# Bias rows and key mask of two attention layers: from one-row fp32 matmuls to one matmul of three or six bf16 rows per bank

## What is computed

```
# layer 0 (8 heads of 32)
xn = LN(x)
q = softmax(xn @ Wq + bq, within a head)
k = softmax(xn @ Wk + bk + (1 - mask) * -1e6, over the tokens)
v = (xn @ Wv + bv) * mask
y = q @ (k^T v per head)
hh = silu(LN(y) * (1 + scale) + shift) @ W_out + b_out
x = x + hh
# layer 2 (16 heads of 16)
q = xn @ q_w + q_b;  k = xn @ k_w + k_b
att = softmax(q k^T + (1 - mask) * -1e6, over the keys)
y = att @ ((xn @ v_w + v_b) * mask)
hh = silu(LN(y) * (1 + scale) + shift) @ out_w + out_b
x = x + hh
```

## Time and profile before

| | us |
|---|---|
| median of 3 runs | 3865.28 (3852.82 to 3866.88) |
| the profiled execution, its span | 3873.2 |
| TensorE busy | 2902.1 (75%) |
| VectorE busy | 2801.5 (72%) |
| ScalarE busy | 2089.7 (54%) |
| GpSimd busy | 1716.0 (44%) |

### The profile page before, as it was taken

How to read it: one execution, slowest core, us unless ns; L and a number is a source line. 1 busy time by engine, 2 the same in 40 slices (tenths; PEclk the granted TensorE clock), 3 DMA queues, 4 the chain that set the end, 5 groups by cost and what they waited for, 6 DMA issues and landing times. The chain is left out here.

```text
span 3873.2 us, 38272 instructions
## 1 busy us (share of the span) xinstructions
PE 2902.1 (75%) x11060; PEld 1488.6 (38%) x11060; DVE 2801.5 (72%) x3410; ACT 2089.7 (54%) x3166; POOL 1716.0 (44%) x1209
## 2 busy tenths in 40 slices
PE   6999667877777877468788878866776866867775
PEld 4555333444444444222333322223434434434443
DVE  1333279999999999755555555515999989999996
ACT  0223267777777777213444444426766756767663
POOL 0000047678677768800000000003767667677686
PEclk7899787988988988768888888768887978878888
DMA  2000111111011101043333333010101011111011
GB/s 78 11 33 22 47 39 44 39 44 50 28 44 50 50 23 55 33 82 63 60 39 66 66 61 61 12 58 33 43 24 60 30 53 50 39 45 61 23 55 49
DMA packets 101857, 176.64 MB, mean 46 GB/s; under 512 B 10219, under 2 KB 88827, under 8 KB 92563
## 3 DMA queue, kind: packets, MB, share of 16 engines
q1 hardware_dynamic: 97430, 161.65, 15.8%
q0 software_dynamic: 4224, 12.59, 1.0%
HBM read 139.69 MB, written 34.12 MB: 45 GB/s over the span
## 5 line engine op out<-in xcount | busy, mean ns | idle before, releaser
L965 POOL TENSOR_TENSOR l_h<-l_h,l_c_all 128x512 f32<-128x512 f32 x1024 | 1483.1, 1465 | 709.6 <-DVE l_h L896 688.5
L896 DVE TENSOR_TENSOR_SCAN l_h<-l_dA,l_ps_dbu 128x512 f32<-128x512 f32 x1024 | 1210.1, 1205 | 137.2 <-PE l_ps_dbu L1089 81.8
L1089 PE MATMUL l_ps_dbu<-ident,l_dub 128*128 128x128 f32 x4096 | 691.8, 303 | 282.8 <-DVE l_h L896 256.9
L767 ACT ACTIVATE l_dub<-l_duT,l_b_tok 128x512 f32<-128x512 f32 x1024 | 723.6, 711 | 281.5 <-PE l_ps_dbu L1089 281.5
L1089 PEld LDWEIGHTS l_ps_dbu<-ident,l_dub 128*128 128x128 f32 x4096 | 520.2, 154 | 783.0 <-DVE l_h L896 535.5
L781 ACT ACTIVATE l_dA<-l_dt,l_a_neg 128x512 f32<-128x512 f32 x1024 | 724.1, 711 | 0.2
L1076 PE MATMUL l_ps_y<-l_h,ident 128*128 128x512 f32 x1024 | 630.2, 702 | 104.5 <-DVE l_h L864 103.9
L1346 DVE TENSOR_REDUCE l_q_max<-l_ring 128x2 f32<-128x1024 f32 x256 | 312.7, 1224 | 335.7 <-PE l_ring L1614 332.9
L1499 ACT ACTIVATE l_probs<-l_ring 128x1024 f32<-128x1024 f32 x256 | 261.7, 1024 | 433.3 <-PE l_ring L1623 432.3
L864 DVE TENSOR_TENSOR l_h<-l_h 128x512 f32<-128x512 f32 x512 | 459.8, 901 | 26.1 <-POOL l_h L965 26.0
L925 POOL DMA_INDIRECT l_x_in<-x_dram,l_idx_x x32 | 33.2, 1038 | 951.8 <-DMA l_idx<-in_idx 938.7
(11 more groups left out here) (181 smaller groups left out, 3049.2 us busy)
## 6 DMA issues: line engine op xcount, KB each, us to landing
l_c_all<-c_rows_dram SPq DMA_DIRECT2D x64, 1024.0 KB, 4.8
l_res<-x_dram SPq DMA_DIRECT2D x24, 512.0 KB, 5.4
parts_dram<-l_parts SPq DMA_DIRECT2D x48, 256.0 KB, 2.8
l_qs<-parts_dram SPq DMA_DIRECT2D x48, 256.0 KB
l_ks<-parts_dram SPq DMA_DIRECT2D x48, 256.0 KB
l_x_in<-x_dram SPq DMA_DIRECT2D x16, 512.0 KB, 5.3
x_dram<-l_res SPq DMA_DIRECT2D x16, 512.0 KB, 3.0
su_cond_w<-in_cond_w SPq DMA_DIRECT2D x1, 5120.0 KB, 15.1
```

The lines of the kernel that those rows point to most:

```text
L767: return act.activation(dub[:, n % 2, t, :], duT[:, p, t, :], ACT.Copy, scale=b_tok[:, p, t, n:n + 1])
L896: dve.tensor_tensor_scan(h[:, h_slot(s), :], dA[:, s % DA_RING, :], ps_dbu[:, dbu_slot(s), :], 0.0, ALU.mult, ALU.add).then_inc(scan_ok, 1)
L965: pool.tensor_tensor(h[:, h_slot(s), :], h[:, h_slot(s), :], c_all[:, (n // C_GROUP) % 2, n % C_GROUP, :], ALU.mult).then_inc(hc_ok, 1)
L1089: last = pe.transpose(ps_dbu[:, dbu_slot(s), t * P:(t + 1) * P], dub[:, n % 2, t, j * P:(j + 1) * P], ident[:])
```

## The change

Before, each bias was added by fp32 matmuls with one row. Now each bias is split into three bf16 parts whose sum is the fp32 value (first part: the value rounded to bf16; second: the rest rounded; third: the rest of that), the parts lie on three partitions (`row_stack`), and one bf16 matmul with three rows of ones as weights adds them to a whole bank of two token tiles. It now stands first in the bank and starts it (start=True); the fp32 matmuls add to it. For k of layer 0, bias and mask go into one matmul of six rows: the left side holds three bias parts over three rows of ones, the right side three rows of ones over three mask parts.

The parts are made once. For layer 0 that happens in the setup: VectorE splits, SyncE moves the parts onto their partitions, the mask's by way of memory. For layer 2 it happens at the layer's start. The load of the rows and the per-batch mask load and mask operation of layer 0 are gone.

```diff
 # setup_block, SyncE
+                sp.dma_start(mask_rest[:], io["mask_k"]).then_inc(mask_in, 16)
                 sp.dma_start(cond_w[:], io["cond_w"]).then_inc(weights_in, 16)
+                sp.wait_ge(mask_split, 5)
+                sp.dma_start(io["mask_parts"], mask_parts[:]).then_inc(mask_st, 16)
+                sp.wait_ge(split, 4)
+                for a in range(3):
+                    sp.dma_start(row_stack[a:a + 1, :], row_parts[:, a, :]).then_inc(stack_in, 16)
+                sp.wait_ge(ones_in, 3)
+                for a in range(3):
+                    sp.dma_start(k_left[a:a + 1, :], row_parts[:, a, D:2 * D]).then_inc(stack_in, 16)
+                sp.wait_ge(mask_st, 16)
+                sp.dma_start(k_right[3:6, :, :], io["mask_parts"].rearrange("b a t -> a b t")).then_inc(stack_in, 16)
+                sp.wait_ge(stack_in, 16 * 7)
                 sp.wait_ge(gate_out, 1)
 # setup_block, GpSimd
+                pool.memset(early["ones_b"][:], 1.0).then_inc(ones_in, 1)
+                pool.memset(k_left[:], 1.0).then_inc(ones_in, 1)
+                pool.memset(k_right[:], 1.0).then_inc(ones_in, 1)
 # setup_block, VectorE, ahead of its wait for TensorE
                 dve.wait_ge(loaded, 48)
+                dve.wait_ge(mask_in, 16)
+                dve.tensor_copy(row_parts[:, 0, :], rows[:, 0:4 * D]).then_inc(split, 1)
+                dve.tensor_scalar(mask_rest[:], mask_rest[:], 1.0, MASKED, ALU.subtract, ALU.mult).then_inc(mask_split, 1)
...
+                dve.tensor_tensor(mask_parts[:, 2, :], mask_rest[:], mask_parts[:, 1, :], ALU.subtract).then_inc(mask_split, 1)
 # linear_attention
-                sp.dma_start(rows[:], io["rows"]).then_inc(w_in, 16)
-                        sp.dma_start(mask_row[:, p, :], io["mask_k"][bass.ds(b, 1), :]).then_inc(mask_ld[p], 16)
-                    dve.wait_ge(mask_ld[p], loads)
-                    dve.tensor_scalar(mask_add[:, p, :], mask_row[:, p, :], 1.0, MASKED, ALU.subtract, ALU.mult).then_inc(madd_ok, 1)
-                def project(dst, src, weight, bias):
-                    for t in range(TB):
-                        for k in range(DH):
-                            pe.matmul(dst[:, t, :], src[:, k, t * P:(t + 1) * P], weight[:, k, :], start=(k == 0), stop=False)
-                        last = pe.matmul(dst[:, t, :], ones[:], bias, start=False, stop=True)
+                def project(bank, src, weight, bias):
+                    for a in range(2):
+                        pe.matmul(bank[:, a, :].rearrange("p (i d) -> p i d", d=D), ones_b[0:3, :], bias, start=True, stop=False, skip_group_check=True)
+                        for i in range(2):
+                            t = 2 * a + i
+                            for k in range(DH):
+                                last = pe.matmul(bank[:, a, i * D:(i + 1) * D], src[:, k, t * P:(t + 1) * P], weight[:, k, :], start=False,
+                                                 stop=(k == DH - 1), skip_group_check=True)
                     return last
-                        pe.matmul(ps_k[:, h, :], row("L0_bk")[:, h * P:(h + 1) * P], ones[0:1, 0:1].to_broadcast([1, T]), start=False, stop=False)
-                        last = pe.matmul(ps_k[:, h, :], ones[:], mask_add[:, p, :], start=False, stop=True)
+                        last = pe.matmul(ps_k[:, h, :], k_left[:, h * P:(h + 1) * P], k_right[:, bass.ds(b, 1), :], start=False, stop=True)
 # softmax_attention, SyncE, ahead of its wait for the mask parts
-                sp.dma_start(rows[:], io["rows"]).then_inc(w_ld, 16)
+                sp.dma_start(rows[:], io["rows"][:, 4 * D:6 * D]).then_inc(rows_ld, 16)
+                sp.wait_ge(split_ok, 4)
+                for a in range(3):
+                    sp.dma_start(row_stack[a:a + 1, :], row_parts[:, a, :]).then_inc(row_stack_ld, 16)
 # softmax_attention: GpSimd fills ones_b first; VectorE, ahead of the mask's split
+                dve.wait_ge(rows_ld, 16)
+                dve.tensor_copy(row_parts[:, 0, :], rows[:]).then_inc(split_ok, 1)
...
+                dve.tensor_tensor(row_parts[:, 2, :], row_rest[:], row_parts[:, 1, :], ALU.subtract).then_inc(split_ok, 1)
 # softmax_attention, TensorE
                 def tokens(bank, src, weight, bias, h):
+                    pe.matmul(bank[:].rearrange("p (i d) -> p i d", d=D), ones_b[:], bias_pair(bias), start=True, stop=False, skip_group_check=True)
                     for t in (2 * h, 2 * h + 1):
                         o = bank[:, (t % 2) * D:(t % 2 + 1) * D]
                         for k in range(DH):
-                            pe.matmul(o, src[:, k, t * P:(t + 1) * P], weight[:, k, :], start=(k == 0), stop=False)
-                        last = pe.matmul(o, ones[:], row(bias), start=False, stop=True)
+                            last = pe.matmul(o, src[:, k, t * P:(t + 1) * P], weight[:, k, :], start=False, stop=(k == DH - 1), skip_group_check=True)
                     return last
                 stage_a(0)
+                pe.wait_ge(ones_ok, 1)
+                pe.wait_ge(row_stack_ld, 48)
```

More of the change, by code:

```diff
@@ L118, in setup_block @@
         rows = sb("su_rows", [1, len(ROWS) * D])
+        row_rest = sb("su_row_rest", [1, 4 * D])
+        row_parts = ctx.enter_context(nc.sbuf_tensor("su_row_parts", [1, 3, 4 * D], BF16))
+        mask_rest = sb("su_mask_rest", [B, T])
+        mask_parts = ctx.enter_context(nc.sbuf_tensor("su_mask_parts", [B, 3, T], BF16))
+        row_stack, k_left, k_right = (early[k] for k in ("row_stack", "k_left", "k_right"))
         loaded, weights_in, filled, diag_done = sem("su_loaded"), sem("su_weights_in"), sem("su_filled"), sem("su_diag")
+        mask_in, split, mask_split, mask_st, stack_in, ones_in = (
+            sem("su_mask_in"), sem("su_split"), sem("su_mask_split"), sem("su_mask_st"), sem("su_stack_in"), sem("su_ones_in"))
         silu_done, mm_done, gate_mm, gate_out, stored, steps = (
@@ L206, in linear_attention @@
         vecs, ident, ones, eps, coef = (keep[k] for k in ("vecs", "ident", "ones", "eps", "coef"))
-        rows = sb("rows", [1, len(ROWS) * D])
+        row_stack, ones_b, k_left, k_right = (early[k] for k in ("row_stack", "ones_b", "k_left", "k_right"))
         w = sb("w", [P, DH, 4 * D])
@@ L240, in linear_attention, with bias_pair @@
             sem("yn_tr"), sem("hT"), sem("o_mm"), sem("res"))
-        def row(name):
+        def bias_pair(name):
             r = ROWS.index(name)
-            return rows[:, r * D:(r + 1) * D]
+            return row_stack[:, r * D:(r + 1) * D].unsqueeze(1).to_broadcast([3, 2, D])
         passed_v, res_free = sem("passed_v"), sem("res_free")
@@ L248, in linear_attention @@
             sem("st"), sem("qmax"), sem("qsum"), sem("qinv"), sem("kinv"), sem("st2"), sem("ln_a"), sem("ln_b"))
-        qv, vv = (bank[:].rearrange("p a (k d) -> p (a k) d", d=D) for bank in (ps_q, ps_v))
+        vv = ps_v[:].rearrange("p a (k d) -> p (a k) d", d=D)
         def batches(eng, body):
@@ L432, in _ @@
             def _(pe):
-                pe.wait_ge(w_in, 48)
+                pe.wait_ge(w_in, 32)
                 def transposed(src):
@@ L453, in project_out @@
                     pe.wait_ge(hT_ok, b + 1)
-                    project(vv, hT, wo, row("L0_b_out")).then_inc(o_mm, 1)
+                    project(ps_v, hT, wo, bias_pair("L0_b_out")).then_inc(o_mm, 1)
                 def body(b, p, has_prev, has_next):
@@ L481, in body @@
                         pe.wait_ge(res_ok, b + 2)
-                    project(vv, xnT, wv, row("L0_bv")).then_inc(v_mm, 1)
+                    project(ps_v, xnT, wv, bias_pair("L0_bv")).then_inc(v_mm, 1)
                     pe.wait_ge(q_ok, b + 1)
@@ L1132, in softmax_attention @@
         vecs, ident, ones, eps, coef = (keep[k] for k in ("vecs", "ident", "ones", "eps", "coef"))
-        rows = sb("rows", [1, len(ROWS) * D])
+        rows, row_rest = sb("rows", [1, 2 * D]), sb("row_rest", [1, 2 * D])
+        row_parts, row_stack, ones_b = sb("row_parts", [1, 3, 2 * D], BF16), sb("row_stack", [3, 2 * D], BF16), sb("ones_b", [3, P], BF16)
         w = sb("w", [P, DH, 4 * D])
@@ L1159, in softmax_attention @@
         ps_x, ps_s, ps_o = (ctx.enter_context(nc.psum_tensor("l2_" + name, [P, T], F32)) for name in ("ps_x", "ps_s", "ps_o"))
+        rows_ld, split_ok, row_stack_ld, ones_ok = sem("rows_ld"), sem("split"), sem("row_stack_ld"), sem("ones")
         w_ld, fill_ok, mask_ok, mask_p1, mask_p2, mask_p3, mask_st = (
@@ L1174, in softmax_attention, with bias_pair @@
         OUT = TB // 2
-        def row(name):
-            r = ROWS.index(name)
-            return rows[:, r * D:(r + 1) * D]
+        def bias_pair(name):
+            r = ROWS.index(name) - ROWS.index("L2_bv")
+            return row_stack[:, r * D:(r + 1) * D].unsqueeze(1).to_broadcast([3, 2, D])
         def rows_of(ap, b):
@@ L1714, in build @@
         }
-        setup_block(nc, io, keep)
-        linear_attention(nc, io, keep)
+        with ExitStack() as front:
```

(9 more changed lines are left out.)

41 lines of the change are left out of this document (28 added, 13 removed).

## The result

The changed kernel takes 3742.4 us (median of 4 runs, 3740.0 to 3752.5); the kernel before took 3861.9 beside it on the same chip (3852.8 to 3866.9). The ratio is 0.969 (95% interval 0.966 to 0.972). The forecast was 3764 us with a range of 3732 to 3800: the time lies in the range, 22 us under the forecast. The profiled execution has a span of 3743.0 us.

A forecast was written before the change was run, and what follows sets the result against it. TensorE was taken to bound the linear period's second half and softmax v/output banks; x DMA and rstd the first half. 34 + 22 + 5 + 41 - 1 = 101 us off 3873.2 gives 3772, less 7.9: 3764 us, range 3732 to 3800.

The forecast's parts named there:

- The price of a bias: Both attention layers: each two-tile token bank gives back 0.92 us at the full clock, 1.75 us at the half clock.
- Rival (e): Bias matmuls: the few-row matmul costs as much as the fp32 bias, 0.62 us; 3784 us, chance 0.03.
- rival (d): Banks on the path: bf16 to fp32 changes stop TensorE; 1.85 us each cancels the gain, 2.4 gives 3903; chance 0.03.
- The period: Linear layer, one residual sum to the next at the full clock: 33.6 us, 5.7 less than 39.28.
- new wait for `hT`: Linear layer, output projection: its input comes late, so TensorE newly waits about 1.2 us.
- the v projection buys nothing: Linear layer, first half of the period: 1.9 us less v work gains nothing; x DMA and rstd steps are late already.
- The clock in the six periods: Linear layer, six full periods: as much lost to the half clock as before, 12 us.
- (a): Linear and softmax layers: the clock rises once one-row passes are gone; 3734 us, chance 0.16.
- (b): Linear layer, every batch: the clock falls into new idle time before the attention matmuls, 25 us more; 3789 us, chance 0.10.
- First and last batch: Linear layer: 22 us gained up to the first residual sum, 5 us behind the seventh.
- Softmax layer: Softmax layer's v and output banks: 14.5 and 26 us gained, together 41 us.
- Rival (c): Softmax layer: half its gain is taken back by VectorE's maxima or a late DMA; 3784 us, chance 0.06.

The follow-up runs named there:

- wide_rows: The kernel before with the one-row fp32 passes of both attention layers made 128 rows high, zeros in the other rows; 3754 us, ratio 0.971.
- only_l2: The kernel before with the change in the softmax layer alone, setup and linear layer left old; 3818 us, ratio 0.989.
- tall_bf16: The changed kernel with its three- and six-row bf16 bias matmuls made 128 rows high by zero rows; 3707 us, ratio 0.958.
- early_x: The changed kernel with each x of the linear layer loaded a second time for the residual sum; 3724 us, ratio 0.966.
- silu_first: The changed kernel with ScalarE's silu moved ahead of the exponential of q in the linear layer; 3742 us, ratio 0.970.
- after_again: The changed kernel run once more with nothing changed, on another chip; 3750 us, ratio 0.967.

## Why the prediction was right, and where its steps were off

**The price of a bias** was the term mis-sized most widely. The forecast took 0.92 us for a token bank at the full clock and 1.75 at the half; the trace gives 3.37 - 2.24 = 1.13 and, in the first batch,

```profile
70.41 0.60 PE L475 MATMUL l_ps_q<-row_stack,ones_b 3*128 3x512 bf16 x1 [1.54 <-ACT l_xnT L434]
70.94 3.78 PE L479 MATMUL l_ps_q<-l_w,l_xnT 128*128 128x256 f32 x8
74.65 0.60 PE L475 MATMUL l_ps_q<-row_stack,ones_b 3*128 3x512 bf16 x1
```

6.3 - 4.24 = 2.06. The bf16 matmul itself was sized right, 0.31 us and 0.53 for 0.32 and 0.55. The error was to take the four 128-row passes, 1.06 us between one-row biases, as the price of 128-row work. It was 0.86, as wide_rows shows, and 0.2 us of it went with the one-row neighbours. With half as many neighbours eight passes take 1.93 us instead of 2.12. Rival (e) had no part in it, and rival (d), a stop of 1.85 us or more at each bank, measured at most 0.3 us (2.24 against 1.95).

**The period.** Forecast 33.6 us at the full clock, found 34.03 less 1.60 in the half-clock q projection = 32.4. The 1.2 us less are 0.5 in q, 0.5 in the output projection (4.39 us from 250.91 to 255.30, for 4.9), and 0.37 from R to q (16.84 for 17.21), less 0.2 in the chain from q to `hT` and behind the output projection. The new wait for `hT` (1.2 forecast, 1.28 found) was right. That the v projection buys nothing in the first half was nearly right, 0.37 us a period, since the prediction read one batch whose x DMA was the slow one.

**The clock in the six periods.** Forecast: as much lost as before, 12 us. Found: 205.6 - 6 x 32.4 = 11 us. That the amount was right is luck, since everything behind it changed. The two long low stretches of before (27.3 us of low clock) are gone, and a short one behind the idle time of each batch has come; rivals (a) and (b) each happened in part and cancelled. Six periods gave 42.4 us for 34: 6 x 6.9 = 41 and the last 1 from the clock. But the old layer's 12 us were themselves chance: in only_l2 its six periods lost nothing (235.7 us), and against that execution the change gave 30 us. The forecast lies between the two.

**First and last batch.** 29.4 us for 22 and 8.1 for 5. In this execution the clock did what rival (a) said, and rose at 76.1 us, ahead of its k block. The step that was off is the taken 22 us, between a clock that stays down and one that rises at k. How much of the rise is the change's own stays open: the same old first batch reached its first residual sum 5.5 us sooner in only_l2, against which the gain is 24 us. What wide_rows, tall_bf16 and the softmax layer's half-clock times carry is weaker than a rule: with more few-row work there was more time at the half clock, though TensorE wasn't less busy.

**Softmax layer.** 52 us for 41. At the measured prices the prediction's own count gives 12 x 1.13 + 2 x 2.06 + 2.5 x 1.13 + 13.5 x 2.06 = 48 us. The remaining 4 lie within the 10 us that this layer moves with the same code; 9 of its 16 output banks ran at the half clock, by the mean of 503 ns of their biases between 380 and 600, where 13.5 did before. Rival (c) didn't happen.

**Setup.** VectorE's split took 7.0 us (3.98 to 10.94), for some 8, and SP's small DMAs passed beside the gates' matmuls. The layer began at 55.5 us, and at 54.6 to 58.2 in the others: nothing that can be measured. The large weight load landed 0.2 us later, as foreseen within 0.4.

The new sum is 80.1 + 52.2 + 1.4 - 3.4 = 130 us between the profiled executions. Medians differ by 120, since the profiled execution of before lay 11.3 us above the 3861.9 us measured beside after and that of after 0.6 above its own. The prediction allowed 7.9 for the first, from its three runs. So the gain in medians is 120 us where 101 were forecast; of the 29 us between the sum's 101 and the profiles' 130, some 13 are the price of a bias (6 in the six periods, 7 in the softmax layer).

**What stays open.** The order of the clock's rises and falls was described, not predicted. early_x and silu_first vary the idle time with the few-row work unchanged, tall_bf16 varies the height, and each moved the low stretches. But the same code also had other stretches in another execution (before and only_l2, after and after_again), and all kernels but after were profiled once. So how much of the gain is the clock's isn't shown, and what brings a fall isn't either. That the 0.39 us is the time of the change itself, and not of the one-row passes, rests on the two forms of the bank (0.79 us with two changes, 0.39 with one), not on a record that shows a stop. Nor was the few-row cost tried at heights between six and 128 rows.

## What to carry to other kernels

A one-row bias or mask matmul costs more than its own passes: put it into one matmul per bank, and make it as high as its neighbours with zero rows, which here was free and worth another 1%. Price a removed instruction by what its neighbours take without it, not by the spacing beside it. And where TensorE has short waits, shortening one can move the half clock onto other work or lift it altogether, so read the granted clock of each stretch before and after, and judge an edit by a sum over several periods and, where the clock moves, by more than one profile.

## What the runs showed of the hardware

- Between one-row and 128-row fp32 passes TensorE lost about 0.2 us per change, back and forth 0.39 us; between three-row bf16 and 128-row fp32 0.3 us for a bank; between bf16 and fp32 at the same height nothing that shows (0.23 us for 512 columns of bf16, 1.72 for eight fp32 passes of 256).
- In before the engine stayed at 1.2 GHz from 56 to 121 us while its records show it busy 46.6 of the 49.5 us from 71.7 on; the same work with 128-row biases (wide_rows) rose to 2.4 GHz at 75.9 us. But with the same layer's code in only_l2 the clock rose at 86.1 us, was low again from 92.9 to 113.4, and then stayed at 2.4 GHz through six periods (235.7 us).
- Two profiles of the same kernel (after, after_again) had the same softmax layer to 0.1 us, and linear layers 6.4 us apart; kernels with the same softmax layer had it at 914, 921 and 924 us, with 361, 378 and 385 us at the half clock.
